# A graph layer whose edges are sorted by a bitonic network: the rows of sorted ranks are dealt to four partition groups that finish the sort alone, and the gather tiles are read from the transposed sort

## The reference

```python
xn = layernorm(x)
h = xn @ W.T + bias
deg = segment_sum(1, src)
h = rsqrt(1 + deg) * h
agg = segment_sum(h[dst], src)          # 100000 rows gathered, summed by src
gnn = rsqrt(1 + deg) * (agg + h)
mix = linear attention of xn (keys' softmax over all nodes), times a gate, @ Wproj
x = x + gnn + mix
x = x + the FFN (256 -> 1024 -> 256, gelu) of layernorm(x) for the 3124 nodes of highest score
```

## Time and profile before

| | us |
|---|---|
| timed runs: median (lowest to highest of 3) | 1440.8 (1437.7 to 1441.14) |
| span of the profiled execution | 2130.4 |
| PE busy (matmuls) / DVE busy in it | 1246.2 / 1027.4 |
| GpSimd busy / ACT busy in it | 798.3 / 370.1 |

### The profile page before, as it was taken

How to read it: one execution, slowest core, us unless ns; L and a number is a source line. 1 busy time by engine, 2 the same in 40 slices (tenths; PEclk the granted TensorE clock), 3 DMA queues, 4 the chain that set the end, 5 groups by cost and what they waited for, 6 DMA issues and landing times.

```text
span 2130.4 us, 30338 instructions
## 1 busy us (share of the span) xinstructions
PE 1246.2 (58%) x6547; PEld 925.5 (43%) x6548; DVE 1027.4 (48%) x3654; ACT 370.1 (17%) x1168; POOL 798.3 (37%) x851
## 2 busy tenths in 40 slices
PE   2679889545636465556545555655464574646663
PEld 2578768433424344334333333433343353434442
DVE  8988999134433333334334333433433353334348
ACT  7426655210100000001000000100000010001010
POOL 0000142535444443534444353453444444445410
PEclk9789999868868677777768777777777787778786
DMA  7001023322222222222222221222222222222213
GB/s 171 2 16 65 30 85 89 105 69 75 67 73 63 74 67 62 77 65 69 69 69 67 62 80 58 69 78 60 74 64 74 65 71 75 64 74 79 64 35 120
DMA packets 88000, 148.71 MB, mean 70 GB/s; under 512 B 31017, under 2 KB 60041, under 8 KB 87327
## 3 DMA queue, kind: packets, MB, share of 16 engines
q0 software_dynamic: 37536, 102.55, 16.5%
q1 hardware_dynamic: 28810, 24.55, 4.3%
q10 hardware_dynamic: 21606, 21.05, 3.3%
HBM read 132.83 MB, written 12.80 MB: 68 GB/s over the span
## 4 chain that ended last, share of the span: by engine, by line
another core or an unknown queue 35%; issue 22%; PE 21%; DVE 11%; ACT 5%; SPq 4%; ACTq 1%; DMA 1%; DVEq 0%; POOL 0%
PE bank L857 7%; PE bank L802 5%; SPq L352 2%; PE bank L731 2%; PE bank L739 2%; DVE big_t L963 2%; ACT keyB L589 2%; PE bank L723 1%; PE bank L825 1%; DVE keyB L1008 1%; DVE keyA L1008 1%; DVE big_g L1404 1%; DVE keyA L1007 1%; DVE keyB L1007 1%
## 5 line engine op out<-in xcount | busy, mean ns | idle before, releaser
L419 POOL DMA_INDIRECT gath<-table,idx_stage x782 | 745.5, 953 | 944.4 <-SPq L354 660.0
L1211 DVE TENSOR_SCALAR onehot<-iota_b,row_of,minus_row 128x128 bf16 x978 | 272.0, 316 | 579.5 <-issue 384.1
L857 PE MATMUL bank<-w_sb,keyB 128*125 128x256 f32 x800 | 283.0, 530 | 398.5 <-ACT keyB L589 398.5
L857 PEld LDWEIGHTS bank<-w_sb,keyB 128*125 128x125 f32 x800 | 214.7, 276 | 483.6 <-ACT keyB L589 435.7
L802 PE MATMUL bank<-gath,onehot 128*128 x978 | 291.7, 409 | 192.8 <-SPq L351 95.2
L847 PE MATMUL bank<-vv,w_sb 128*128 128x125 f32 x1600 | 220.3, 290 | 129.1 <-issue 127.7
L802 PEld LDWEIGHTS bank<-gath,onehot 128*128 x978 | 95.1, 97 | 378.5 <-issue 274.8
L847 PEld LDWEIGHTS bank<-vv,w_sb 128*128 128x128 f32 x1600 | 205.4, 206 | 111.3 <-issue 109.5
L589 ACT ACTIVATE keyB<-bank,b_sb 128x125 f32<-128x125 f32 x400 | 108.0, 379 | 714.5 <-remote 690.6
L1241 DVE SCALAR_TENSOR_TENSOR WT<-bank,norm,WT 125x256 f32<-125x256 f32 x50 | 24.2, 484 | 340.2 <-ACT WT L597 172.3
L597 ACT ACTIVATE WT<-bank,norm 125x256 f32<-125x256 f32 x50 | 23.7, 473 | 785.0 <-issue 427.4
(11 more groups left out here) (281 smaller groups left out, 1540.3 us busy)
## 6 DMA issues: line engine op xcount, KB each, us to landing
gath<-table,idx_stage POOLq DMA_INDIRECT x782
onehot<-in_x ACTq DMA_DIRECT2D x50, 125.0 KB
parts<-table ACTq DMA_DIRECT2D x50, 125.0 KB
h_s<-in_x ACTq DMA_DIRECT2D x50, 125.0 KB
big_g<-in_x SPq DMA_DIRECT2D x5, 1120.0 KB
table<-parts SPq DMA_DIRECT2D x50, 112.0 KB
out<-big_g SPq DMA_DIRECT2D x8, 560.0 KB
w_sb<-in_L_ffn_w SPq DMA_DIRECT2D x2, 1024.0 KB
```

Source lines behind the costliest of these rows:

```text
L419: g.indirect_dma_start(out=gath[:, j, :], out_offset=None, in_=table[:, :], in_offset=bass.IndirectOffsetOnAxis(ap=idx_stage[:, j:j + 1], ...
L857: last = t.matmul(bank[7][0:P, 0:C], hid[:, k, :], w2_sb[:, k, :], start=k == 0, stop=k == HC - 1)
L1211: last = nc.vector.tensor_scalar(onehot_g[:, slots, u * 128:(u + 1) * 128].rearrange("p a r -> p (a r)"), iota_b[:, :], row_of[:, bass.ds( ...
```

## The change

1. **Edges on 128 partitions.** 781 edges lie on each of 128 partitions; the 32 that are left go one by one to the first 8 partitions of each group of 32, and the columns up to 784 are pads. The histogram's pieces have 196 columns.
2. **The deal.** The local sort goes down to the last stage, which writes the ranks of a partition grouped by rank mod 4 (`by_hand`). Sixteen DMAs, 11 from the sync queue and 5 from GpSimd, give each of the four groups of 32 partitions a quarter of every partition's ranks. The norms, the split of h's row (rowsh) and the signal for them are moved behind this point. DVE waits for the deal.
3. **Four sorts of 32 partitions.** Levels 9 and 10 are done again on the dealt rows, then five levels (m = 1 to 5) within each group. The levels m = 6 and 7 are gone. `turn_lanes` flips half of the columns in the transposed layout. In levels 4 and 5 the stages stay transposed and end at distance 32, so that the last layout holds the sorted keys in runs of 32 along the partitions.
4. **Tiles from the transposed sort.** A tile is 32 consecutive keys from each of the four groups. `col_of` and `row_of` are taken from the sort's own buffer; PE's eight transposes and DVE's copies are gone. A first piece of 64 columns is done first.
5. **Bounds from the tiles.** After the tables DVE transposes the sorted keys, takes the smallest and largest of each run, compares them with the 49 window bounds and counts; a matmul at row block 47 (KEYS_AT) adds the counts over each group; DVE takes minimum and maximum over the groups. `first_block`, `end_block` and a new `made_row`, the number of visits made before a window, come from it. PE's and DVE's loops load a third register per window. The sync queue stores the first indices ahead of its wait for these bounds; PE's first sums wait for them.
6. **Constants.** 24 row blocks are held (a third copy, from gath), HIST_AT = (2, 11, 20), ten peeks within the histogram instead of seven, LAG = 3.

```diff
-EP, EC = 125, EDGES // 125
+EP, GROUPS, LANES = 128, 4, 32
+EC = 784
-LAG = 2
+LAG = 3
-MERGE_DOWN_TO = {4: 3, 5: 4, 6: 6, 7: 8}
+LEVELS_IN_GROUP = 5
+STAY_TURNED = 4
+HAND_BY_SYNC = 11
-PEEK_FROM, PEEK, PEEK_LEAD = 7, 12, 20
+PEEK_FROM, PEEK, PEEK_LEAD = 10, 12, -15
-HELD = 16
-HIST_AT = (3, 9, 15)
+HELD = 24
+HIST_AT = (2, 11, 20)
-KEYS_AT = 37
+KEYS_AT = 47
...
+        def deal(eng, g, c, done):
+            to = (c + g) % GROUPS
+            eng.dma_start(dealt_keys[to * LANES:(to + 1) * LANES, g * HAND:(g + 1) * HAND],
+                          ranked_keys[g * LANES:(g + 1) * LANES, c * HAND:(c + 1) * HAND]).then_inc(s[done], 16)
...
-            histogram(1, between=statistics)
-            lead(LEADS[0], LEADS[1])
+            histogram(1, between=((P // 2, statistics),))
+            lead(LEADS[0], LEADS[0] + 5)
             peek()
-            histogram(2, between=peek)
+            lead(LEADS[0] + 5, LEADS[1])
+            histogram(2, between=((0, peek), (41, peek), (83, peek)))
...
+            for k, e in upper[:-1]:
+                local_stage(k, e, 0, COLS)
+            by_four = a[:, :].rearrange("p (r h two) -> p h two r", h=2, two=2)
+            by_hand = b[:, :].rearrange("p (h two r) -> p h two r", h=2, two=2)
+            exchange(by_four[:, :, 0, :], by_four[:, :, 1, :], by_hand[:, :, 0, :], by_hand[:, :, 1, :])
+            v.sem_inc(s["ranked"], 1)
             v.wait_ge(s["hist"], NHIST + 1)
             nc.vector.tensor_copy(deg[:, :], bank[3][0:P, 0:NW]).then_inc(s["nwt"], 1)
...
+            split_row(rows_h, "wtp", 1)
+            v.sem_inc(s["rowsh"], 1)
+            v.wait_ge(s["dealt"], 16 * HAND_BY_SYNC)
+            v.wait_ge(s["dealtp"], 16 * (len(hands) - HAND_BY_SYNC))
+            for k, e in upper:
                 local_stage(k, e, 0, COLS)
-            for m in range(1, 8):
-                turn(m)
-                if m >= 7:
...
-                swap_blocks()
-                for e in range(min(m, 5) - 1, -1, -1):
-                    distance(1 << e)
-                swap_blocks()
-                for e in range(LOGF - 1, MERGE_DOWN_TO.get(m, 0) - 1, -1):
+            for m in range(1, LEVELS_IN_GROUP + 1):
+                if m <= STAY_TURNED:
+                    swap_blocks()
+                turn_lanes(m)
+                for e in range(m - 1, -1, -1):
+                    distance(1 << e)
+                if m < STAY_TURNED:
+                    swap_blocks()
+                for e in range(LOGF - 1, (4 if m >= STAY_TURNED else -1), -1):
                     distance(1 << e)
-            v.sem_inc(s["sortd"], 1)
-            v.wait_ge(s["keyp"], 1)
...
                 if m == KEYS_AT:
-                    t.wait_ge(s["sortd"], 1)
-                    for b in range(COLS // 128):
-                        last = t.transpose(bank[2 + b // 4][:, (b % 4) * 128:(b % 4 + 1) * 128],
-                                           sorted_keys[:, b * 128:(b + 1) * 128], ident[:, :])
-                    last.then_inc(s["keyp"], 1)
+                    t.wait_ge(s["counted"], 1)
+                    t.matmul(bank[3][:, 64:64 + 2 * (NW - 1)], heads[:, :], tiles_below[:, :, :].rearrange("p a w -> p (a w)"),
+                             start=True, stop=True).then_inc(s["cntp"], 1)
...
+                before = t.value_load(made_row[0:1, bass.ds(w, 1)], min_val=1, max_val=DUE_MAX)
...
-                    made = q + (2 * w + 1)
+                    made = q + before
```

More of the change, by code:

```diff
@@ L239, in gps_layer @@
         coef = spent[:, 10 * NW:11 * NW]
[L241 to L243 removed]
+        names = ("edges wload wmain const const2 wtp wev hotr hist stats normd rowsh wss wsc diag nwt bn bna bg1 kps cntp chain "
+                 "counted tabs final issued outs xn tp hid main hgv gtp ghT gps gate hev split xstore "
+                 "moved kT kmaxd cntd kmt kmx kmr kv ekv xnr ctxp sumcp sumtp sumtc vdone ctxn wqcp wqcd pads ranked dealt dealtp oh arrived visits freed due duerow selfused "
                  "op og pp xb xm sum xh low x1 st nt zed ge zwt ztp zT hp gelu yp yv base halves csum").split()
@@ L326, in _ @@
             sp.dma_start(w2_sb[:, :, :], w2.rearrange("(c p) n -> p c n", p=128)).then_inc(s["wload"], 16)
-            sp.wait_ge(s["due"], 1)
-            sp.wait_ge(s["gate"], NW)
-            sp.dma_start(due_row[0:1, :].rearrange("a (i k) -> a i k", k=ROUND), visits_due[0:NROUND, :]).then_inc(s["duerow"], 16)
+            sp.wait_ge(s["ranked"], 1)
+            for g, c in hands[:HAND_BY_SYNC]:
+                deal(sp, g, c, "dealt")
             def table_rows(m):
@@ L436, in _ @@
             ]
+            a.wait_ge(s["pads"], 2)
+            for to, of in ((e_int, src_s), (col_of, dst_s)):
+                for g in range(GROUPS):
+                    a.dma_start(to[g * LANES:g * LANES + SPARE, EW:EW + 1], of[g, :, :]).then_inc(s["edges"], 16)
             for to, of in first:
@@ L1172, in _ @@
[L1172 to L1180 removed]
+            assert cur[0] is tile_keys
@@ new lines, in _ @@
+            last.then_inc(s["counted"], 1)
+            v.wait_ge(s["cntp"], 1)
+            tiles = other[:, 0:2 * (NW - 1)].rearrange("p (a w) -> p a w", a=2)
+            step(nc.vector.tensor_copy(tiles, bank[3][:, 64:64 + 2 * (NW - 1)].rearrange("p (a w) -> p a w", a=2)))
+            for half in (64, 32):
+                for n, side in ((0, ALU.min), (1, ALU.max)):
+                    step(nc.vector.tensor_tensor(tiles[0:half, n, :], tiles[0:half, n, :], tiles[half:2 * half, n, :], side))
@@ new lines, in _ @@
+            begin, end, shared, upto, whole = (tile_keys[0:LANES, n * 64:n * 64 + NW] for n in range(5))
+            whole_i = whole[:, 0:NW - 1].bitcast(I32)
+            step(nc.vector.tensor_scalar(whole_i, tiles[0:LANES, 0, :], 0.5, -0.25, ALU.mult, ALU.add))
+            step(nc.vector.memset(begin[:, 0:1], 0.0))
+            step(nc.vector.tensor_scalar(begin[:, 1:NW], whole_i, float(NBLK - 1), None, ALU.min))
+            step(nc.vector.tensor_scalar(whole_i, tiles[0:LANES, 1, :], 0.5, 0.25, ALU.mult, ALU.add))
@@ L1188, in _ @@
+            v.wait_ge(s["due"], 1)
             for n in ("x1", "og", "yv"):
```

207 lines of the change are left out of this document (116 added, 91 removed).

## The result

The changed kernel takes **1453.43 us** (median of 4 runs, 1447.65 to 1454.13) beside 1439.57 for the kernel before in the same job (4 runs, 1437.7 to 1441.14): ratio 1.0093, 95% interval 1.007 to 1.0116. It is 14 us slower (1%), where the prediction had 1406 us, 34 us faster.

What follows compares the result with a forecast made beforehand. It took GpSimd's 782 gathers as the bound, its undisturbed ledger giving 1429.4 us for the kernel before. From the measured 1440.8 it took 35 us for an earlier gather 29: 1406 us, range 1384 to 1424.

Steps and rivals of the forecast that it cites:

- the part on DVE until the first index table: DVE's work from histograms to first index table: table at 342 instead of 383.85 us, first gather 42 us earlier.
- The deal: Sixteen transfers of 32 KB beside norms and row split: DVE waits 2.4 us for them (0 to 15).
- rival D: The change doesn't reach the loop's start, through a slow deal or longer DVE wait: 1438 to 1442 us, chance 0.04.
- Bound and cadence: In the window loop, 782 gathers on GpSimd, 1.25 us apart, bind: 977.5 us, 19.55 us a window.
- The stages behind it: DVE's sort behind the deal: 116.2 us of work plus 16.7 us beside GpSimd's subtractions.
- The keys stage: PE's stage ahead of gather 29: starts at 258 us, 21 us earlier, and ends at 388 undisturbed.
- Rival B: Gathers slow ACT and PE in the keys stage, moving gather 29 only 15 to 25 us: 1416 to 1426, chance 0.14.
- The bounds: Window bounds from DVE and PE's matmul at m = 47: due at 385 us, cost 0, up to 5.
- The visits: Window and block pairs in the loop: 444 instead of 489, gaining nothing beside 782 unchanged gathers.
- The gathers beside DVE's bounds: Gathers starting while DVE counts tiles are not held up: 0; the skill's rule would give some 5 us.
- Rival C: Dealt tiles make each gather dearer: gain gone from 0.045 us a gather, 1468 us at 0.08; chance 0.04.
- The third register load: One more load per window on PE and DVE, ahead of a wait: 0, at most 50 x 0.25 = 12 us.

Runs made afterwards that it cites:

- e2: Changed kernel with histogram pieces of 200, 200, 200 and 184 columns instead of four of 196: 1434.18 us, ratio 0.9931 to the kernel before.
- e3: Changed kernel with the eight spare-edge transfers and the wait for pads moved from ACT's queue to the sync queue: 1447.14 us, ratio 1.0024 to the kernel before.
- e4: Changed kernel with both edits, the histogram pieces of e2 and the moved transfers of e3: 1418.14 us, ratio 0.9818 to the kernel before.
- after: The changed kernel as it was made, in its profiled execution: 1454.13 us, span 1452.4 us.
- e1: The kernel before, unchanged, profiled again: 1444.86 us, span 1443.1 us.
- e5: The kernel of e4 with every window also summing the block behind its last one, 49 visits more: 1997.69 us beside 2152.65 for the kernel before.
- e6: The kernel of e4 with two spare-edge transfers instead of eight: 1996.32 us beside 2152.65 for the kernel before.
- e7: The kernel of e4 with 20 PE matmuls with zeros ahead of each block wait in the last window: 1995.52 us beside 2152.65 for the kernel before.
- e13: The kernel of e5 once more, 49 visits more than e15: 1425.32 us beside 1414.68 for e15.
- e15: The kernel of e4 in a later job: 1414.68 us, ratio 0.9836 to the kernel before.
- e12: The kernel of e4 once more, on a chip where the kernel before takes 2154.4 us: 1999.91 us.
- e14: The kernel of e4 with one spare-edge transfer per list and the 20 zero matmuls of e7 in the last window: 1414.83 us beside 1414.68 for e15.

## Why the prediction was wrong

The step that failed stands in the part on DVE until the first index table: **"ten peeks instead of seven lie within the histograms, so I let them end at 146 in both"**. They end at 184.4. In it two costs were left at nothing that the diff shows: the comparisons' new shape (49 blocks; 28.7 us of DVE's time, e2) and the eight transfers with a wait ahead of ACT's loads (10.2 us at the first gather, e3). Undone together they give 1415 to 1418 us; 1406 lay 9 to 12 below, and the direction would have been right. What e4 still shows above the sum is a first gather at 352.8 instead of 347, 7.9 us of waits for slots at gathers 29 and 49, and a tail 4 us longer.

The Trainium skill (Vector Engine (DVE) Microarchitecture Reference, Performance modes — why throughput varies by op and dtype) says that an op on one source takes four 16-bit elements per cycle only if, among other conditions, the outermost dimension of its operands is even, or odd and equal in both. 49 blocks on the one side, and on the other 196 columns that touch and so may count as one run, are a case for it. By the Trainium skill's page falling to two per cycle would add some 51 ns, an estimate (49 cycles more at the 0.96 GHz that it gives); e2 and after show 41. The runs show that 49 blocks are dear and 50 or 46 are not; that this rule is the reason is argued, not shown. The prediction did not weigh it, and what it bears on is the larger of the two costs.

The other steps, in their order:

- *Bound and cadence*: right. 782 gathers, 1.25 us apart where nothing lies between, in e1 and in after; the ledger took this for the mean, which is 1.27.
- *The rest up to the ranks*: right. In e4 the histograms end at 146.7 us (146) and the ranks are there at 201.9 (200).
- *The deal*: DVE waits 2.5 us for it (2.4 expected). So rival D fell by its cause; what it said of the result, a gain that doesn't reach the loop's start, came by another way.
- *The stages behind it*: 138.9 us (248.6 to 387.5) instead of 132.9. The sum lacked a wait of 5.5 us: the row split in the middle of the stages stands still for ACT. The contention with GpSimd's subtractions was about right: the 148 half stages are busy 117.4 us beside 102.6 at the undisturbed 0.693, so 14.8 (16.7 expected).

```profile
DVE rows_b L1005 <- ACT lnb_wide L585: 5.5, 1, 5.5
DVE keyB L1042 <- DMA keyA<-keyB: 2.5, 1, 2.5
DVE keyA L1218 <- PE bank L788: 17.1, 1, 17.1
```

```profile
387.53 1.56 DVE L1194 TENSOR_SCALAR col_of<-keyB 128x64 int32<-128x64 int32 x2
```

- *The keys stage*: 299 instead of 258 us, late by the same 41; vdone at 429.0 instead of 388. Rival B (15 to 25 us) fell: in e1, after and e4 gather 29 waits 0, 2.2 and 3.4 us. Only in e5, e6 and e7 does it wait 23 us.
- *The bounds*: DVE waits 17.1 us for the matmul at m = 47, and they are due at 426.7; their row must still reach the sync queue. "0 (up to 5 if m = 47 slips)" held: gather 29 waits 2.2 us. Gather 49 waits 4.5 more, which the prediction lacked: PE's first visit is at 431.9, 40 us behind the first gather (25 in e1), and slots come free late.
- *The visits*: 458 (916 matmuls), not 444. Why the count from the inputs was 14 short was not looked into. "They gain nothing" was nearly right: 49 visits cost 10.6 us (e13).
- *The gathers beside DVE's bounds*: 0 was right. Their mean is 961 ns, 964 in e1. The Trainium skill's rule against this (SBUF — State Buffer, Who interferes with whom), as the prediction used it for copies and tensor_scalars, does not show in that mean. Single gathers are held, but by another form: the fourth and sixth take 1.47 and 2.10 us, and each starts while DVE runs a TENSOR_TENSOR of its counting (L1208) and ends 0.8 us behind it; in e2, e4 and e15 two gathers do the same. That is 1.7 us. Rival C fell as well.

```profile
398.63 1.79 DVE L1208 TENSOR_TENSOR keyB<-keyB,bound_row 128x1568 bf16<-128x1568 f32 x1
399.14 2.10 POOL L447 DMA_INDIRECT gath<-table,idx_stage  x1 [0.30 <-issue]
```

- *The tail*: taken as equal in both. It is 65.3 us from the last gather's start instead of 61.2, by PE's idle time and the clock.
- *The third register load*: 0.30 us on PE's queue (median of 50), above the 0.25 that the prediction took for its bound. What it costs was not isolated by a run.

Of the trace of before, the prediction's "distorted" was right as a warning and wrong as a cause: the timed runs of e5 to e12 take as long, without a profile.

## What to carry to other kernels

When a change touches the shape of an operand that hundreds of instructions share, cost those instructions again, even when the diff shows only a constant: look whether a count of blocks or rows turned odd. Small transfers put ahead of large loads on a queue are paid by whoever waits for the last load, not by their own bytes. An edit far from the bound may carry a larger cost than the gain at it; two such costs that meet at one wait show up in full only when both are taken away.

## What the hardware showed beyond that

- A DVE comparison of bf16 against a constant, 128x196 in 49 blocks of 4, comes every 0.163 us; 128x200 in 50 blocks every 0.122; 128x184 in 46 blocks every 0.119; 125x200 in 25 blocks of 8 every 0.166.
- PE's matmul with a 128x50 moving operand takes 230 ns with elements 8 bytes apart and 277 with 16.
- Two loads of 1 KB and less took 11.45 and 9.67 us to issue on ACT's queue at 11.7 and 23.2 us, when all of x had been asked for, and 0.5 us each at 4.7 and 5.3 us (e4).
- An idle time of PE of 2.47 us was followed by 5.4 us at a granted clock of 0.50, the level of 1.2 GHz (after); with PE kept busy it stayed at 1.00 (e14).
- A gather that starts beside a DVE TENSOR_TENSOR of 128x1568 float32 elements ends 0.8 us behind it: 1.4 to 2.4 us instead of 0.95 (after, e2, e4, e15).
